# Half-size mix units in a written-out order, and part 1's first loads behind half of the first mix

## What is computed

```python
def _L0_rec_ref(feature, weight):            # feature (512, 200, 64), weight (200, 64, 64), float32
    bilinear = jnp.einsum('bie,ied->bid', feature, weight)
    out = jnp.einsum('bid,bjd->bij', bilinear, feature)
    return out                               # (512, 200, 200), float32
```

## Time and profile before

| | |
|---|---|
| median of three runs | 310.88 us |
| profiled execution | 306.8 us |
| its span, first to last instruction | 305.0 us |
| granted TensorE clock, mean | 0.961 |
| PE busy | 243.2 us |
| DVE busy | 152.8 us |
| ACT busy | 130.1 us |
| POOL busy | 12.5 us |
| mean DMA rate | 368 GB/s |

### The profile page before, as it was taken

One profiled execution on the slowest core, in us unless ns is written; L12 is line 12 of the kernel. 1 busy time (PEld: TensorE's weight loads), 2 busy tenths in 40 slices (PEclk: granted clock), 3 DMA queues, 4 the chain that ended last, 5 costly groups with the idle time before them and its releaser, 6 DMA issues.

```text
span 305.0 us, 14640 instructions
## 1 busy us (share of the span) xinstructions
PE 243.2 (80%) x6800; PEld 210.9 (69%) x6800; DVE 152.8 (50%) x180; ACT 130.1 (43%) x181; POOL 12.5 (4%) x23
## 2 busy tenths in 40 slices
PE   6839849999877586999867785898985774998990
PEld 2437749888776476878866675866885674996970
DVE  0153634556755443537644454634765554775621
ACT  2153515445544324245444243542653451665420
POOL 2004800000000000000000000000000000000000
PEclk9996997999999979899999799999999999999997
DMA  7999997999999999968999999986999999599995
GB/s 219 415 417 357 363 410 302 324 376 373 369 360 416 407 419 420 409 280 354 374 366 408 383 411 417 388 355 248 389 371 391 408 387 417 210 402 381 409 408 218
DMA packets 22172, 112.35 MB, mean 368 GB/s; under 512 B 4320, under 2 KB 4320, under 8 KB 21856
## 3 DMA queue, kind: packets, MB, share of 16 engines
q1 hardware_dynamic: 22112, 111.43, 92.6%
HBM read 29.49 MB, written 81.92 MB: 365 GB/s over the span
## 4 chain that ended last, share of the span: by engine, by line
PE 76%; issue 16%; DMA 2%; SPq 2%; DVE 1%; ACT 1%
PE psum L322 50%; PE psum L285 17%; PE psum L339 8%; DMA w_sb<-w_dram 2%; SPq L166 2%; PE psum L305 1%; DVE tile L355 1%; ACT mixed L376 0%; ACT w_sb L390 0%; SPq L178 0%
## 5 line engine op out<-in xcount | busy, mean ns | idle before, releaser
L322 PE MATMUL psum<-x_sb,mixed 64*64 64x200 f32 x3072 | 163.1, 351 | 14.0 <-issue 12.5
L322 PEld LDWEIGHTS psum<-x_sb,mixed 64*64 64x64 f32 x3072 | 133.3, 139 | 27.9 <-issue 17.9
L355 DVE COPY tile<-psum 128x800 f32<-128x800 f32 x100 | 99.2, 992 | 88.6 <-PE psum L322 79.8
L355 ACT COPY tile<-psum 128x800 f32<-128x800 f32 x100 | 82.4, 826 | 70.2 <-PE psum L322 54.0
L285 PE MATMUL psum<-x_sb,w_sb 64*64 64x64 f32 x3072 | 64.4, 221 | 35.1 <-issue 34.2
L285 PEld LDWEIGHTS psum<-x_sb,w_sb 64*64 64x64 f32 x3072 | 61.7, 134 | 40.5 <-issue 37.7
L376 ACT COPY mixed<-psum 64x512 f32<-64x512 f32 x48 | 27.8, 580 | 43.2 <-PE psum L285 42.6
L376 DVE COPY mixed<-psum 64x512 f32<-64x512 f32 x48 | 33.1, 689 | 16.7 <-PE psum L285 15.5
L378 ACT COPY mixed<-psum 128x512 f32<-128x512 f32 x24 | 14.1, 586 | 36.3 <-PE psum L285 36.2
L378 DVE COPY mixed<-psum 128x512 f32<-128x512 f32 x24 | 16.6, 691 | 22.3 <-PE psum L285 22.2
L339 PE MATMUL psum<-x_sb,tails 128*32 128x200 f32 x512 | 25.0, 342 | 0.1
(11 more groups left out here) (5 smaller groups left out, 1.7 us busy)
## 6 DMA issues: line engine op xcount, KB each, us to landing
out_dram<-tile SPq DMA_DIRECT2D x192, 400.0 KB, 5.6
x_sb<-x_dram SPq DMA_DIRECT2D x64, 400.0 KB, 6.9
out_tail_dram<-tile SPq DMA_DIRECT2D x8, 400.0 KB, 4.2
w_sb<-w_dram SPq DMA_DIRECT2D x1, 1152.0 KB, 15.2
w_sb<-w_dram SPq DMA_DIRECT2D x4, 256.0 KB, 7.3
w_sb<-w_dram SPq DMA_DIRECT2D x1, 1024.0 KB, 13.1
```

The source lines that it names most:

```text
L322: last = nc.tensor.matmul(psum[half_rows(pair), n % BANK_PAIRS * 2 + h, a * FIELDS:(a + 1) * FIELDS], mixed[half_rows(h), (CHUNKS * g + c) ...
L355: copy(tile[:, k % SLOTS, engine], psum[:, bank:bank + 2, 0:2 * FIELDS]).then_inc(copied[engine], 1)
```

## The change

Four things change.

1. `BANK_FIELDS` is 4 instead of 8, so a mix unit has 8 fields, fills half of each of its two banks, and a chunk has 8 mix units instead of 4. The layout of W and its cuts stay as they were, with their own constants (`W_FIELDS`, `W_UNITS`); a mix unit waits for W only if it is the first of the two that share a cut's 16 fields.
2. The order within a block is written out as a string for each block: s is a score unit, m a mix unit, t a tail unit and x the tail mix. The strings differ from group to group.
3. In SP's queue a wait for the fourth mix unit stands ahead of part 1's first loads, and chunk 1's W (cut 4) is issued behind two of these eight loads instead of behind all.
4. Which pieces of part 1 are waited for by score units, and which by a mix unit, is worked out from the strings (`WAITED`: 2, 3, 2 and 2 pieces).

```diff
-BANK_FIELDS = BANK // HALF_SAMPLES
+BANK_FIELDS = BANK // HALF_SAMPLES // 2
 MIX_FIELDS = 2 * BANK_FIELDS
 MIX_UNITS = CHUNK // MIX_FIELDS
...
-MIX_AFTER = (1, 3, 5, 6)
...
+ORDER = (
+    ("ssmsmsmssmssmsssmsmsmxsss", "ssmsssmssmstmtmsmsmsssmsss", "ssmsmsssmsmsmsmssmssmsss"),
...
+CROSSING = (PART - CHUNK) // MIX_FIELDS
+WAITED = [-(-"".join(order[0].split("m")[:CROSSING + 1]).count("s") // (2 * PIECE_TILES)) for order in ORDER]
...
-            for n in range(X_LOADS):
+            sp.wait_ge(unit_ready, MIX_UNITS // 2)
+
+            for n in range(X_STRIPS):
                 load_part1(sp, 0, n)
-            for n in range(MIX_UNITS, len(W_CUTS) - 1):
-                load_w(n)
+            load_w(W_UNITS)
+            for n in range(X_STRIPS, X_LOADS):
+                load_part1(sp, 0, n)
+            load_w(W_UNITS + 1)
...
-                if g == 0 and c == 0:
-                    pe.wait_ge(w_loaded[m], 16)
+                w_unit, later = divmod(m * MIX_FIELDS, W_FIELDS)
+                if g == 0 and c == 0 and not later:
+                    pe.wait_ge(w_loaded[w_unit], 16)
...
-                source = psum[:, n % BANK_PAIRS * 2 + swap, :].rearrange(
+                source = psum[:, n % BANK_PAIRS * 2 + swap, 0:BANK_FIELDS * HALF_SAMPLES].rearrange(
```

More of the change, by code:

```diff
@@ L49 @@
 STRIP_STORES = STRIPS * 16
+W_FIELDS = 16
 W_OWN = FIELDS // 2
-OWN_FIELDS = MIX_FIELDS // 2
-W_CUTS = [OWN_FIELDS * n for n in range(MIX_UNITS)] + [CHUNK // 2, CHUNK, W_OWN]
+OWN_FIELDS = W_FIELDS // 2
+W_UNITS = CHUNK // W_FIELDS
+W_CUTS = [OWN_FIELDS * n for n in range(W_UNITS)] + [CHUNK // 2, CHUNK, W_OWN]
 def own_index(field):
-    unit, r = divmod(field, MIX_FIELDS)
-    own = min(MIX_FIELDS, FIELDS - unit * MIX_FIELDS) // 2
+    unit, r = divmod(field, W_FIELDS)
+    own = min(W_FIELDS, FIELDS - unit * W_FIELDS) // 2
     return r // own, unit * OWN_FIELDS + r % own
@@ L82, in walk @@
         for c in range(CHUNKS):
-            for t in range(TILES):
-                for u in range(2):
-                    score(n, g, c, t, u)
-                    n += 1
-                if c == TAIL_CHUNK[g] and t in TAIL_AFTER[g]:
-                    tail(n, g, TAIL_AFTER[g].index(t))
-                    n += 1
-                to, chunk = next_chunk(g, c)
-                if t in MIX_AFTER and to < GROUPS:
-                    mix(n, to, chunk, MIX_AFTER.index(t))
-                    n += 1
-                if c == 0 and t == TAIL_MIX_AFTER:
+            to, chunk = next_chunk(g, c)
+            done = {"s": 0, "m": 0, "t": 0, "x": 0}
+            for kind in ORDER[g][c]:
+                k = done[kind]
+                done[kind] += 1
+                if kind == "s":
+                    score(n, g, c, k // 2, k % 2)
+                elif kind == "m":
+                    mix(n, to, chunk, k)
+                elif kind == "t":
+                    tail(n, g, k)
+                else:
                     tail_mix(n, g)
-                    n += 1
+                n += 1
 def count_copies():
@@ L218, in _ @@
             done = 0
-            units = list(range(MIX_UNITS, CHUNKS * MIX_UNITS))
-            for unit in units[:MIX_UNITS] + [CHUNKS * MIX_UNITS] + units[MIX_UNITS:]:
+            units = list(range(W_UNITS, CHUNKS * W_UNITS))
+            for unit in units[:W_UNITS] + [CHUNKS * W_UNITS] + units[W_UNITS:]:
                 own = slice(unit * OWN_FIELDS, min((unit + 1) * OWN_FIELDS, W_OWN))
-                pool.wait_ge(w_loaded[MIX_UNITS if unit < 2 * MIX_UNITS else MIX_UNITS + 1], 16)
+                pool.wait_ge(w_loaded[W_UNITS if unit < 2 * W_UNITS else W_UNITS + 1], 16)
                 for h in range(HALVES):
@@ L266, in mix @@
                     wait_part0(g)
-                if g == 0 and c == 0:
-                    pe.wait_ge(w_loaded[m], 16)
+                w_unit, later = divmod(m * MIX_FIELDS, W_FIELDS)
+                if g == 0 and c == 0 and not later:
+                    pe.wait_ge(w_loaded[w_unit], 16)
                     for e in range(2):
-                        pe.wait_ge(w_crossed[e], m + 1)
-                elif g == 0:
-                    pe.wait_ge(w_crossed[2], 2 * ((c - 1) * MIX_UNITS + m + 1 + (c > 1)))
-                if first <= PART < first + MIX_FIELDS:
-                    for p in range(4 * LAST_WAITED // PIECE_QUADS + 1, PIECES):
+                        pe.wait_ge(w_crossed[e], w_unit + 1)
+                elif g == 0 and not later:
+                    pe.wait_ge(w_crossed[2], 2 * ((c - 1) * W_UNITS + w_unit + 1 + (c > 1)))
+                if m == CROSSING and c == 1:
+                    for p in range(WAITED[g], PIECES):
                         wait_part1(g, p)
@@ L313, in score @@
                     wait_copies(NUMBER["mix", g, c, MIX_UNITS - 1])
[L314 to L315 removed]
+                if c == 0 and u == 0 and t % PIECE_TILES == 0 and t // PIECE_TILES < WAITED[g]:
+                    wait_part1(g, t // PIECE_TILES)
                 for a in range(2):
@@ L385, in tail_mix @@
                 copy(tails[half_rows(engine), :, 0:4:3, engine, :], source).then_inc(copied[engine], 1)
-            for n in range(MIX_UNITS):
+            for n in range(W_UNITS):
                 own = slice(n * OWN_FIELDS, (n + 1) * OWN_FIELDS)
```

15 lines of the change are left out of this document (7 added, 8 removed).

## The result

The changed kernel's median is 309.95 us over 12 runs (306.99 to 316.37), against 309.99 us for the kernel before over its 12 (308.45 to 311.99). The ratio to the kernel before is **1.0101, with a 95% interval of 1.006 to 1.0142**: about 3 us slower. The ratio compares undisturbed executions only, while the medians take all. So the loss is 3 to 4 us by the ratios and 0 to 1.3 us by the medians. Single executions of one kernel scatter by up to 4%, and an effect of 1 us is never clear here.

A forecast was written before the change was run, and what follows sets the result against it. PE was taken to run at the pace of its code, a 256-instruction block about every 6 us while DMA is full. Start -2.0, late banks +0.5, spread units -1.9 gave -3.4 us: 307.5 us on the median's scale, range 301.5 to 313.

The forecast's parts named there:

- rival C: Chunk 1: PE's lead fills DMA, so code comes every 6 us and eats the lead; gain 0 to 1, 310.4 us, chance 0.27.
- PE reaches chunk 1 about 2 us earlier: Group 0: the lead from an earlier score 0 lasts through chunk 0 until PE starts chunk 1; about 2 us.
- the hole pays for both: Group 0's chunk 1: 3.6 us unused DMA time covers PE 2 earlier plus DMA 1.7 later; -2.0 us at chunk 2.
- part 3: Half-size mix units and new order, all blocks: +0.5 us for late banks, -1.9 us for units spread out.
- PE's wait for W: Group 0, after two scores: PE waits 1 us for chunk 1's W, hidden below the next code block.
- DMA time unused: At the start, through the late part 1 loads: 2.4 us of unused DMA time added, bounds 1.5 and 3.5.
- Score 0: First score unit of group 0: starts at 20.8 instead of 22.78 us, 2.0 us earlier, bounds 0 and 2.3.
- The code stall of 3.59 us: First mix, 16.89 to 20.48 us: code comes sooner through an emptying queue, 2.2 us off the stall, bounds 0 and 3.5.
- +0.5 for late banks: Dense runs of units: four bank pairs span less work, so banks come late now and then; +0.5 us, bounds 0 and 3.8.
- rival A: Chunk 1: DVE's added copies reach banks and mixed rows late; slower by 3.8 to 11 us, up to 314.7, chance 0.07.
- -1.9 for spread units: Chunk 1 of groups 1 and 2: spread units bring tiles more evenly; -1.9 us, between 0 and 4.4.
- B: Start: late loads only cost, code comes no sooner, DMA and chain 1.7 to 2.4 us late; 312 to 313 us, chance 0.11.

The follow-up runs named there:

- f1: The changed kernel without SP's added wait, chunk 1's W still behind two part 1 loads: 308.64 us, ratio 1.0023 to the kernel before.
- f0: The changed kernel run again, nothing altered: 311.40 us, ratio 1.014 to the kernel before.
- e4: The kernel before with half of the stored bytes left out (all tiles but the last store ACT's half alone): 276.79 us, one execution.
- h1: The kernel before with the next group's part 0 loads moved to chunk 0's last two tiles and chunk 1's first six: 311.44 us, ratio 1.0125.
- e2: The changed kernel with SP's queue at the start as in the kernel before: 308.67 us, ratio 0.9998 to the kernel before.
- f3: The changed kernel with SP waiting for all eight units of the first mix instead of four: 314.84 us, ratio 1.0242 to the kernel before.
- e1: The kernel before with only the change's start (SP's wait, early W), old units and order: 310.47 us, ratio 1.004.
- g2: The kernel before with only chunk 1's W moved behind two part 1 loads, no wait: 310.23 us, ratio 1.0106.
- e3: The kernel before with 8-field mix units in pairs at the old places, old start: 307.23 us, ratio 0.9942.
- h0: The kernel before with 8-field mix units in pairs at the old places, a repeat of e3: 308.60 us, ratio 0.9964.
- g4: The kernel before with 8-field units spread evenly, the same order in all groups, old start: 309.55 us, ratio 1.0056.
- k2: The kernel before with half as many mixing matmuls, each twice as wide, 12 code blocks less, output partly wrong: 296.28 us, ratio 0.9664.

## Why the prediction was wrong

The sum of -3.4 us forecast a gain; by ratio the change cost 3.1. The median, 309.95 us, lies within the stated range and near rival C's 310.4, but by no merit of the sum.

**What failed is the account of PE's lead, in two steps.** The first is "PE reaches chunk 1 about 2 us earlier". PE began to score 1.4 us earlier and reached chunk 1 at 50.18 us, 0.4 later than before. On its way stood the 3.78 us for chunk 1's W, taken as 1 us and hidden, and a chunk 0 in which DMA was full all the time (share 1.00), since its loads came late. f1, without the wait, is there at 46.81.

The second is "the hole pays for both". It took the idle DMA time of group 0's chunk 1 as slack that swallows DMA's lateness and pays PE's lead out. At the start of chunk 1 f0 and the changed kernel are 4.1 and 3.4 us behind f1, at its end 3.2 and 3.4, and in the changed kernel (1 - 0.83) x 24.73 = 4.2 us of DMA time went unused in it, as against 3.6 before. By the prediction's own reading PE runs at the pace of its code while DMA is full; it drew that conclusion for the long stretches and for rival C, and not for the hole. The hole is where PE catches up: half idle DMA there means PE at its own speed (e4: 22.5 to 23.9 us), and a fuller one means code stalls (h1: 27 to 28 us). In the changed kernel DMA is full in that block up to 64 us (shares of 0.95 to 1.02 in the windows from 48 on, where the kernel before has 0.61, 0.79, 0.93 and 1.02), PE has a stall of 1.5 us in it, and the hole comes after. That this is why nothing was given back is argued from e4, e2 and h1; no run isolates it.

f1, f0 and f3 give the price: 3.4 us for the wait, 3.3 more for one that ends 3.7 us later. The prediction's -2.0 is therefore about +3, which is most of the miss; the missing -1.4 of part 3 (e2, the same without the new start, is at 0.9998) is the rest. What share of the 3 us is idle DMA and what share PE's wait for W is not shown, nor why the wait added nothing in the kernel before (e1 against g2).

**Terms of the start, one by one.** DMA time unused: 2.4 forecast, 3.6 measured (bounds 1.5 and 3.5, just outside); the 0.7 us of 24 to 28 us did fill up (share 1.01). Score 0: 20.8 forecast, 21.42 measured, so 1.4 us of lead and not 2.0. The code stall of 3.59 us: gone, where 2.2 of it were forecast. PE's wait for W: 1 us, hidden, was forecast; it was 3.78 us, on the path, because the loads were costed at 0.41 MB/us and the windows after the idle time have 205 and 275 GB/s, so POOL had W at 25.5 instead of 21.9 us and PE at 26.9 instead of 23.2. The row that could have warned stood in the trace of the kernel before, where the first loads run alone (columns as in the earlier trace rows):

```profile
4.00:8.00 4.00, 4.00 (x6) 1.48 (x5) 0.00 (x0) 0.19 (x1) 0.00 (x0) 1.00 0.94 309
```

Only the next window, 8 to 12 us, has 410 GB/s.

**Part 3.** The copy was 422 ns, as worked out. The +0.5 for late banks is not seen in e3 and h0, which are, if anything, faster than the kernel before, and rival A is out. The -1.9 for spread units has the wrong sign if it has one: e2 is at 0.9998 against e3's 0.9942 on the same chip, with intervals that overlap, and g4 at 1.0056 on another. Its bound of 4.4 us was taken as stall and low clock; in e4 the same two stretches have only 1.2 us in which PE does nothing, and are still 2.3 us longer in sum than twice group 0's. And the reason it gave for the difference, two mixes and the tail mix just ahead, stands ahead of group 0's chunk 1 too. That no gain came in the long stretches (sum 138.2 against 140.8 us) was nearly right; they gave 2.5 us, and chunk 1 took 5.0 and the end 1.8. But one of them, at 42.48 us, is below the 45 to 48 that the prediction allowed.

**Rivals.** B said that late loads only cost, and gave 312 to 313; it had the right part, sign and size, but one of its two conditions did not hold, since the code block did come sooner. C's mechanism (PE's lead makes DMA full and full DMA makes code slow) is seen in e2, 29.47 us for a block that C priced at 30; in the changed kernel the lead was gone before that block. C priced the whole at nothing. The two belonged together, with more than 0.38 between them. Of the signs, "first score at 20.5 to 21.5", "first long stall under 2 us" for code and "53 packets" were right; "chunk 1 share above 0.9", "W crossing at about 23" (25.5) and "below 23.5 us" did not come, and of the signs against it "chunk 1 above 24 us with code stalls in it" did (24.73 us, one stall of 1.5).

**The page's rule.** That code fetch is mostly hidden (the Trainium skill, Runtime: NRT & Kernel Launch, Instruction fetch mechanics) does not hold for this kernel: with 12 blocks fewer (k2) the waits of 46.7 us fall to 1.0 and the time by 3.4%. Its block size of 256 instructions agrees with the packets and with the spacing of the stalls.

## What to carry to other kernels

When an engine's stalls come at a fixed count of instructions, count its instructions before its work: fewer and longer instructions may be worth more than any order. Idle time of a resource beside an engine that is late is not slack by itself: ask what that idleness speeds up, and move something into it (h1) before crediting anything to it. A wait put ahead of loads may be paid in full, as here in the changed kernel; see what it delays before counting what it frees.
